# GpSimd's job loop: the gather for four jobs on is issued ahead of the scatter instead of behind it

## The reference

```python
x = x + attention(layernorm(x))      # decay scan over k and k*v, 16 heads of 32, w_qkv, w_out
x = x + moe(layernorm(x))            # per token: shared part + its best 2 of 8 experts

# moe, for token rows x:
scores = softmax(x @ gate_w)                       # 8 experts
topk_w, topk_idx = top_k(scores, 2)                # comb = weights at the chosen experts, else 0
g = silu(einsum('td,edh->teh', x, w_gate)) * einsum('td,edh->teh', x, w_up)     # h = 352
routed = einsum('teh,ehd,te->td', g, w_down, comb)
shared = silu(x @ sw_gate) * (x @ sw_up) @ sw_down                              # h = 704
out = routed + shared
```

## Time and profile before

| | |
|---|---|
| median of 3 runs | 739.93 us (736.96 to 740.67) |
| profiled execution, device time | 738.84 us |
| its span, first to last instruction | 736.8 us |
| mean granted TensorE clock | 0.977 |
| busy: PE, DVE, ACT, POOL | 655.2, 441.9, 235.7, 215.4 us |
| job loop, first to last scatter issued | 483.6 to 727.3 us |

### The profile page before, as it was taken

One profiled execution on the slowest core, in us unless ns is written; L12 is line 12 of the kernel. 1 busy time (PEld: TensorE's weight loads), 2 busy tenths in 40 slices (PEclk: granted clock), 3 DMA queues, 4 the chain that ended last, 5 costly groups with the idle time before them and its releaser, 6 DMA issues.

```text
span 736.8 us, 11499 instructions
## 1 busy us (share of the span) xinstructions
PE 655.2 (89%) x3677; PEld 422.1 (57%) x3678; DVE 441.9 (60%) x808; ACT 235.7 (32%) x353; POOL 215.4 (29%) x234
## 2 busy tenths in 40 slices
PE   3979889879899599899998999999899899989982
PEld 2757567558577365465655656655455555545551
DVE  6879888987997661786876976433322232232221
ACT  4343421242342212446665664411111111111110
POOL 6100111101102026333432333143344433334431
PEclk9999999999999799899999999999999999999998
DMA  6840003512433577975855316367666666676662
GB/s 215 280 127 16 15 19 83 161 39 58 117 84 86 132 170 205 273 179 149 183 150 147 58 29 79 66 114 129 128 118 121 120 120 123 125 128 118 118 96 39
DMA packets 111235, 86.87 MB, mean 118 GB/s; under 512 B 79280, under 2 KB 86448, under 8 KB 111200
## 3 DMA queue, kind: packets, MB, share of 16 engines
q1 hardware_dynamic: 88848, 43.94, 25.0%
q0 software_dynamic: 12272, 27.34, 20.8%
q10 hardware_dynamic: 10080, 15.14, 6.8%
HBM read 44.45 MB, written 23.33 MB: 92 GB/s over the span
## 4 chain that ended last, share of the span: by engine, by line
DMA 33%; PE 31%; DVE 16%; issue 12%; ACT 2%; POOL 2%; SPq 2%; POOLq 1%; DVEq 0%; ACTq 0%
DMA out_dram<-y_job,job_tok 26%; PE ring L378 12%; PE ps_y L504 5%; PE ps_g L504 5%; PE ps_u L504 5%; DMA shared<-in_L_attn_w_out_dram 2%; DVE run_kv L1205 1%; DMA routed<-in_L_ffn_w_down_dram 1%; DVE routed L1347 1%; DVE run_kv L1197 1%; SPq L771 1%; PE turn_h L524 1%; DVE run_k L1193 1%; DVE xn L1167 1%; DMA x_in<-in_L_attn_x_dram 1%
## 5 line engine op out<-in xcount | busy, mean ns | idle before, releaser
L1287 DVE TENSOR_TENSOR hidT<-turn_h,hidT 128x384 f16<-128x384 f32 x71 | 39.5, 556 | 129.4 <-ACT hidT L1036 129.2
L911 POOL DMA_INDIRECT out_dram<-y_job,job_tok x39 | 61.4, 1574 | 142.1 <-DVE y_job L1638 74.8
L504 PE MATMUL ps_g<-routed,x_in 128*128 x468 | 76.5, 313 | 17.1 <-DMA x_in<-x_job 17.0
L378 PE MATMUL ring<-xnT_h,wq_h 128*128 128x512 f32 x192 | 81.1, 422 | 11.3 <-DVE run_kv L1197 4.2
L1032 ACT ACTIVATE silu<-ps_g,job_silu 128x352 f32<-128x352 f32 x39 | 21.6, 553 | 209.1 <-PE ps_g L504 209.1
L504 PE MATMUL ps_y<-routed,hidT 128*128 x351 | 82.1, 379 | 1.3 <-DVE hidT L1287 1.3
L378 PE MATMUL ring<-xnT_l,wq_h 128*128 128x512 f32 x192 | 78.1, 407 | 0.0
L378 PE MATMUL ring<-xnT_h,wq_l 128*128 128x512 f32 x192 | 77.9, 406 | 0.0
L836 POOL TENSOR_SCALAR var_eps<-mean_var 128x1 f32<-128x1 f32 x32 | 11.7, 367 | 226.4 <-DVE mean_var L1268 125.7
L504 PE MATMUL ps_u<-routed,x_in 128*128 x468 | 76.2, 313 | 0.0
L504 PE MATMUL ps_y<-shared,hidT 128*128 128x512 f16 x288 | 69.3, 387 | 7.5 <-DVE hidT L1287 7.4
(11 more groups left out here) (222 smaller groups left out, 1062.9 us busy)
## 6 DMA issues: line engine op xcount, KB each, us to landing
routed<-in_L_ffn_w_gate_dram ACTq DMA_DIRECT2D x7, 704.0 KB, 4.8
routed<-in_L_ffn_w_up_dram ACTq DMA_DIRECT2D x7, 704.0 KB, 9.0
x_res<-in_L_attn_x_dram SPq DMA_DIRECT2D x18, 256.0 KB, 3.2
out_dram<-x SPq DMA_DIRECT2D x16, 256.0 KB, 3.3
xn_scratch<-xn_hl SPq DMA_DIRECT2D x16, 256.0 KB, 2.5
out_dram<-y_job POOLq DMA_DIRECT2D x16, 256.0 KB, 4.2
x_in<-in_L_attn_x_dram SPq DMA_DIRECT2D x14, 256.0 KB, 2.7
routed<-in_L_ffn_w_down_dram ACTq DMA_DIRECT2D x7, 512.0 KB, 10.8
```

What stands on the lines that cost most here:

```text
L378: ins = pe.matmul(ps, a, b, start=(i == 0), stop=(i == len(steps) - 1))
L504: ins = pe.matmul(ps, a[i][:, k, :], w(j, k), start=(start and q == 0), stop=(stop and q == len(steps) - 1))
L911: pool.indirect_dma_start(out[:, :], bass.IndirectOffsetOnAxis(job_tok[:, r:r + 1], 0), y_job[:, b, :], None, compute_op=ALU.add).then_inc ...
L1287: dve.tensor_tensor(hidT[:, 1], turn_h[:, 0:FC, :], hidT[:, 0], ALU.subtract).then_inc(s["hidT_s"], 1)
```

## The change

In the job loop of GpSimd the two calls change places. No call is added or removed, and each call keeps its waits.

```diff
             for r in range(JOBS):
-                scatter(r)
                 if r + AHEAD < JOBS:
                     gather(r + AHEAD)
+                scatter(r)
```

## The result

| | before | after |
|---|---|---|
| median of 4 runs each | 738.71 us (736.96 to 740.67) | 720.68 us (717.31 to 722.54) |
| ratio, with its 95% interval | | 0.9743 (0.9706 to 0.9781) |
| profiled execution; its span | 738.84; 736.8 us | 722.54; 720.7 us |
| first scatter issued | 483.6 us | 485.5 us |
| gate product 4 to gate product 38 | 494.36 to 714.94: 6.49 us a job | 495.84 to 698.92: 5.97 us a job |

The account below looks back on a forecast made before the run. Scatter chain and rows for TensorE were taken to bind at 6.49 us a job; at TensorE's own 5.92, 34 jobs gain 19.5 us, from the median 739.93 to 720.4, predicted as 720.5 us, range 717 to 735.

Parts of the forecast that it names:

- Two loops neck and neck: Job loop before the change: scatter after scatter, and rows for TensorE, both bind; gates 6.49 us apart, TensorE's own work 5.92.
- chain of scatters: First loop: each scatter waits for the one before to land; 5.6 us landing plus 0.79 us turnaround, 6.4 us a job.
- collision: In the old order each transpose begins about 0.3 us behind a scatter, costing that scatter about 1 us.
- second loop: Rows for TensorE: scatter r, gather r + 4, its transpose, then gate product r + 4; TensorE waited 17.0 us for rows.
- Gathers a job earlier: GpSimd's gather r + 5 follows scatter r; its wait for transpose r + 3 delays it at most 0.8 us.
- Scatters land at 4.8 us: Deciding step: with transposes 2.9 us behind, scatters take 4.8 us (bounds 4.5 to 6.0), so 5.6 with turnaround, under 5.92.
- The sum: Gate 4 at 494.15 plus 34 jobs of 5.92 us puts gate 38 at 695.4 against 714.94: gain 19.5 us.
- bounds for slow transfers: Slowest transpose taken as 5.67 us and slowest gather as 6.3 us, against more than 8 us from up product to gate.
- Rival A: Scatters over 5.13 us fall behind TensorE and the old 6.4 us pace returns: about 738.5 us; chance 0.13.
- Rival C: Transpose settles 1 to 2.5 us behind a scatter, which could take 6.3 us: 760 us, milder form 750; chance 0.07.
- slope of rows 3 and 4: Old trace's scatter landings by transpose position: 5.20 us at 0.22 ahead, 5.75 at 0.47 behind, 6.02 at 0.71 behind.
- What the doubled result tile takes up: A single late scatter of 5.6 us delays one scatter by 0.5 us, which the doubled `y_job` takes up.

Follow-up runs that it names:

- old order with two targets: The kernel before, with odd jobs adding their rows to a second tensor, so a scatter waits only for the scatter two jobs back: 734.36 us.
- four buffers: The changed kernel with four instead of two buffers for gathered rows, so a gather waits for the transpose four jobs back: 720.28 us.
- new order run again: The changed kernel itself, unaltered, measured again beside the follow-up kernels: 720.72 us.
- turn after down: The changed kernel, with the transpose of job r also waiting for the down product of job r - 3: 718.86 us; with the short pause too, 718.59 us.
- long pause: The changed kernel with a memset of 1536 elements on GpSimd between a scatter's waits and the scatter: 757.24 us.
- five ahead: The changed kernel with each gather one more job ahead, gather r + 5 in front of scatter r: 721.64 us.
- short pause: The changed kernel with a small memset (about 0.2 us) on GpSimd between a scatter's waits and the scatter: 728.74 us.
- turn in scatter: The four-buffer kernel, with the transpose of job r waiting for a mark GpSimd sets behind scatter r - 3 in its program: 727.44 us.

## Why the prediction was right, point by point

- *Two loops neck and neck, TensorE's work the floor under them.* Shown. Freeing the chain of scatters alone gives 4 us, rows in time with the collision kept (727.44) give 11, both give 18 (the 11 are a little low by the slow register loads of that kernel). One size was less good: in the old order with two targets the second loop needed 6.4 us a job, where my expectation for that kernel had 6.15. And the collision was steadier in the prediction than in the trace: the transposes nearest to a scatter stood from 0.22 us ahead to 0.71 behind, median 0.30, not 0.3 every time.
- *Gathers a job earlier, their wait free, transposes released by TensorE.* Shown by the waits and by four buffers. The size was off: a gather was to go at most 0.8 us late, and in the profiled execution single ones waited up to 3.4 us. It cost nothing.
- *Scatters land at 4.8 us once the transposes are out of their start.* The deciding step, taken from the adds of the shared part; the median was 4.8 us. That the collision, and not something else of the old order, had made them slow is shown by the transpose held 0.12 us ahead. The lower end of my bound, 4.5 us with nothing beside it, was one of three such scatters at the end of the trace before; the others took 4.9 and 4.7. So the 4.8 of the new order is what a scatter takes undisturbed.
- *The sum, and luck in it.* 720.5 against 720.68 us is closer than the sum was. It had a gain of 19.5 us, and 18.0 was measured; but it took the gain off 739.93, the median of three runs, where four gave 738.71. The two errors cancel. Gate 38 was to start at 695.4 us and started at 698.92. Of these 3.5 us, 1.7 came ahead of gate 4 (495.84 instead of 494.15; the first scatter was 1.9 us later in this execution), and 1.8 from 5.97 us a job instead of 5.92. A part of that is a term that I had left out, the register load: at 512.7 us of the new order's trace it took 1.19 us, and the gate behind it, at 514.55, stood idle for 0.84. The turn after down kernel, whose longest load from 490 to 690 us was 0.47 us, runs at 5.92.
- *The bounds for slow transfers were too low, without harm.* I had let transposes take at most 5.67 us and gathers 6.3, the slowest before. In the new order run again one transpose took 8.0 and one gather 7.9. The slack from up product to gate, 8.2 us in the trace of the new order run again, only just covered them: the gate behind the transpose of 8.0 us started 0.2 us after it had landed.
- *Rival A* had its threshold right: the long pause crossed it. *Rival C* stood on a wrong reading: I had drawn the slope of rows 3 and 4 on to 1 to 2.5 us behind, where most scatters in fact land at 4.5 to 5.3 us; only those that also have a gather beside that transpose took up to 6.35. By the rule of the Trainium skill that I had put beside rival A ("DMA: Bandwidth & Descriptors", "Queues, rings and completion order"), such late transposes could hold a scatter's landing. Those 2.7 to 3.0 us behind don't: the scatters land at 4.8 us. Whether the rule is at work in the single late landings is open.
- *"What the doubled result tile takes up"* was right for five ahead, where all scatters run 3.5 us behind their results at no cost per job.

## What to carry to other kernels

When a step is moved in a queue, ask not only whether its own waits end in time, but what it will then be issued beside: here some 5 to 7 of 18 us came from a transfer that no longer started together with another. Idle time of an engine put down to "issue" is a hint to look at what its own queue does there, such as the load of a register, and how far behind another engine's DMA it stands. Here a loop held up by a DMA that follows another loop's DMA locked the two in step, and the same collision came nearly every time; releasing one of them by the compute engine unlocked it. To bound a transfer in a place that the trace doesn't show, look for its like in another stage, with the same bytes, operation and neighbour.

## What the runs showed of the hardware that I had not expected

- A transpose of 256 KB alone costs a 256 KB scatter with addition much only if it is issued within a narrow band around the scatter's start: 4.9 us landing at 0.69 us ahead, 5.3 at 0.12 ahead, 6.0 at 0.71 behind (6.65 in one case at 0.77), 5.1 at 1.0, 5.0 at 1.3.
- Gather and transpose issued 0.21 us apart: 8.0 us for the transpose, where the median is 4.3. The scatter ahead of a pair 0.26 us apart landed at 6.1 us in the short pause's trace, and 10 of 12 with such a pair 1.9 to 2.4 us behind took 5.5 to 6.35. The cause is open.
- TensorE's load of one number into a register takes 0.30 us, but up to 1.4 us in some jobs (a median of 0.64 us in the turn in scatter kernel). It stands between the matmuls of two jobs, and it held eight gates for 5.3 us in the short pause kernel. In 63 of 64 cases in which it began 2.1 to 2.87 us behind a scatter's start it was slow, with or without a transpose near. Why is open.
- GpSimd's mark, a nop ahead of the scatter in its program, released SyncE's transpose 0.69 us before the scatter's row begins, and one behind the scatter in its program still 0.12 us before: in these two kernels a semaphore that GpSimd sets beside a DMA did not tell when that DMA's own row begins.
